# Position MLP of a four-layer conv/attention network: layer three in double calls, and one y word table written by halves

## The reference, cut to what matters

```
pos = grid_q[:, :, None, :] - grid_kv[:, None, :, :]          # 16 x 1024 x 64 x 2
bias = jnp.sign(pos) * jnp.log1p(jnp.abs(pos))
bias = jax.nn.relu(bias @ cpb_w1 + cpb_b1)                    # 2 -> 128
bias = jax.nn.relu(bias @ cpb_w2 + cpb_b2)                    # 128 -> 128
bias = (bias @ cpb_w3 + cpb_b3).reshape(b, GROUPS, H * W, Hd * Wd)   # 128 -> 1
sim = jnp.einsum('bhid,bhjd->bhij', qh, kh) + bias
```

## Time and profile before

| | us |
|---|---|
| median of three runs (2898.54 to 2902.41) | 2899.04 |
| time of the profiled execution | 2898.61 |
| its span, first to last instruction | 2896.8 |
| first y matmul of `stage_bias`, from the span's start | 131.0 |
| last layer-three matmul of `stage_bias` | 2038.4 |
| one group of 32 rows | 117.7 |

### The profile page before, as it was taken

One profiled execution on the slowest core, in us unless ns is written; L12 is line 12 of the kernel. 1 busy time (PEld: TensorE's weight loads), 2 busy tenths in 40 slices (PEclk: granted clock), 3 DMA queues, 4 the chain that ended last, 5 costly groups with the idle time before them and its releaser, 6 DMA issues. The chain is left out here.

```text
span 2896.8 us, 45091 instructions
## 1 busy us (share of the span) xinstructions
PE 2738.6 (95%) x19977; PEld 1342.3 (46%) x19977; DVE 2176.3 (75%) x1159; ACT 1650.0 (57%) x2588; POOL 100.8 (3%) x65
## 2 busy tenths in 40 slices
PE   7399999999999999999999999999799999999893
PEld 3333333333333333333333333333478888757551
DVE  5499999999999999999999999998542221234447
ACT  2466776767767777677676776766432222211335
POOL 0000000000000000000000000000422000000004
PEclk9699999999999999999999999999899999999997
DMA  1110000100001001000010000000600000200001
GB/s 68 40 38 14 23 22 16 34 14 23 29 11 34 21 16 36 14 23 22 17 34 14 23 29 10 27 5 1 192 1 0 1 0 1 83 0 1 1 1 58
DMA packets 37603, 72.21 MB, mean 25 GB/s; under 512 B 20960, under 2 KB 21920, under 8 KB 35744
## 3 DMA queue, kind: packets, MB, share of 16 engines
q1 hardware_dynamic: 37344, 69.19, 7.4%
q0 software_dynamic: 64, 0.13, 0.0%
HBM read 60.45 MB, written 8.86 MB: 24 GB/s over the span
## 5 line engine op out<-in xcount | busy, mean ns | idle before, releaser
L731 PE MATMUL l_ps<-mlp_w,W2H 128*64 128x512 f16 x8192 | 1369.1, 393 | 20.1 <-DVE mlp_w L760 20.1
L760 DVE TENSOR_TENSOR mlp_w<-words_x,words_y 128x4096 f32<-128x4096 f32 x256 | 1131.3, 4420 | 0.0
L803 ACT ACTIVATE mlp_w<-l_ps 128x512 f32<-128x512 f32 x1024 | 611.0, 597 | 470.2 <-PE l_ps L731 431.1
L731 PE MATMUL l_ps<-mlp_w,W2L 128*64 128x512 f16 x4096 | 804.0, 389 | 0.0
L731 PEld LDWEIGHTS l_ps<-mlp_w,W2H 128*64 128x64 f16 x8192 | 455.3, 108 | 555.0 <-issue 117.4
L748 DVE SCALAR_TENSOR_TENSOR mlp_w<-relu_bottom,sign_ratio,mlp_w 128x2048 f32<-128x2048 f32 x256 | 601.4, 2349 | 109.0 <-ACT relu_bottom L803 106.7
L803 ACT ACTIVATE relu_bottom<-l_ps 128x512 f32<-128x512 f32 x1024 | 613.0, 599 | 71.1 <-PE l_ps L731 1.4
L731 PEld LDWEIGHTS l_ps<-mlp_w,W2L 128*64 128x64 f16 x4096 | 228.9, 109 | 181.4 <-issue 0.7
L706 PE MATMUL l_ps<-mlp_w,W 128*32 128x512 f32 x2048 | 272.8, 605 | 2.1 <-DVE mlp_w L748 2.1
L719 PE MATMUL l_ps<-y_rows,y_weights_halves 12*128 12x512 bf16 x2048 | 202.5, 385 | 12.5 <-DMA y_rows<-y_pieces 12.5
L719 PEld LDWEIGHTS l_ps<-y_rows,y_weights_halves 12*128 12x128 bf16 x2048 | 51.6, 91 | 336.6 <-ACT relu_bottom L803 232.7
(11 more groups left out here) (339 smaller groups left out, 2410.0 us busy)
## 6 DMA issues: line engine op xcount, KB each, us to landing
table_pos<-pos_table SPq DMA_DIRECT2D x64, 512.0 KB, 3.7
mlp_w<-in_mlp_w SPq DMA_DIRECT2D x8, 1024.0 KB, 8.7
X<-in_x SPq DMA_DIRECT2D x8, 512.0 KB, 7.7
bias_scratch<-bias_rows SPq DMA_DIRECT2D x64, 64.0 KB, 2.0
mlp_w_hi<-bias_scratch SPq DMA_DIRECT2D x16, 256.0 KB, 6.7
out<-Q SPq DMA_DIRECT2D x8, 512.0 KB, 2.7
y_rows<-y_pieces SPq DMA_DIRECT2D x192, 12.0 KB
xn_b<-in_out_wT SPq DMA_DIRECT2D x1, 1024.0 KB, 8.4
```

Source lines behind the costliest of these rows:

```text
L731: last = nc.tensor.matmul(out[q][a * DH:(a + 1) * DH, :], w[:, half], h[a][:, :, k], start=False, stop=stop, tile_position=(0, a * DH))
L760: nc.vector.tensor_tensor(hw[i % 3].rearrange("p r (m j) -> p r m j", j=J), words_x.unsqueeze(1).to_broadcast([P, 2, W, J]), words_y[:, 2 ...
L803: nc.scalar.activation((tops, bots)[d][i % 2][:, r, BANK * u:BANK * (u + 1)], banks[BANK_OF[c % PER]][:], ACT.Relu).then_inc(relu, 1)
```

## The change: what it does

- PE calls layer three after each even pair but the first (after rows 1, 5, 9, ... of a `bg`) for the two pairs before it, instead of once after each odd row. `tops` has three buffers instead of two; the third takes the place in memory of a freed table.
- The x table still exists twice, the y table once. The first half of the y table (y rows 0 to 15) of the next `bg` is written after row 19 once `h1` of the first eight pairs is done; the second half after row 3 of the next `bg` itself. The x jobs come after rows 7 and 11. The `low` parts follow: `h1` pairs 6, 8, 12, and pair 4 of the next `bg`. DVE waits for three jobs at pair 0 and for the fourth at pair 8.
- ACT waits for layer three of pair `i - 3` before it writes a top buffer, and for the fold of pair `i - 2` before it writes a bottom buffer.
- SyncE issues the store of a group before, not after, job 0's coordinates and the y rows of the `bg` after next.

```diff
-    tab = [[sb(f"words_{a}{i}", [P, COLS]) for a in "xy"] for i in range(2)]
+    tab_x, tab_y = [sb(f"words_x{i}", [P, COLS]) for i in range(2)], sb("words_y", [P, COLS])
-    tops = [room([P, 2, TWO]) for _ in range(2)]
+    tops = [room([P, 2, TWO]) for _ in range(2)] + [sb("relu_top", [P, 2, TWO])[:]]
...
+    def words_of(bg, job):
+        a, half = divmod(job, 2)
+        return hi_lo((tab_y[:] if a else tab_x[bg % 2][:])[:, half * HALFC:(half + 1) * HALFC])
...
                     for job in range(1, JOBS):
                         coords(bg + 1, job)
+                store(bg)
                 if bg + 2 < BG:
                     coords(bg + 2, 0)
                     y_rows(bg + 2)
-                store(bg)
...
-                if r and i:
+                if r and i and i % 2 == 0:
+                    layer_three(i - 2)
                     layer_three(i - 1)
+            layer_three(DBL - 2)
             layer_three(DBL - 1)
...
-                    dve.wait_ge(words, JOBS * (bg + 1))
+                    dve.wait_ge(words, JOBS * bg + 3)
+                if n == PER_BG // 2:
+                    dve.wait_ge(words, JOBS * bg + 4)
...
-                if bg + 1 < BG and n >= 4 and n % 2 == 0 and n < 4 + 2 * JOBS:
-                    low(bg + 1, (n - 4) // 2)
+                if bg and n == 4:
+                    low(bg, 3)
+                if bg + 1 < BG and n in (6, 8, 12):
+                    low(bg + 1, (6, 8, 12).index(n))
...
-                if bg >= 2:
+                if a == 0 and bg >= 2:
                     act.wait_ge(h1, PER_BG * (bg - 1))
+                if a and bg:
+                    act.wait_ge(h1, PER_BG * bg - (PER_BG // 2 if half == 0 else 0))
...
-                    if r == 0 and q == 0 and i >= 2:
-                        act.wait_ge(l3, i - 1)
+                    if r == 0 and q == 0 and i >= 3:
+                        act.wait_ge(l3, i - 2)
+                    if r == 0 and q == 1 and i >= 2:
+                        act.wait_ge(folded, i - 1)
...
-                if bg + 1 < BG and y >= 3 and y % 4 == 3 and y < 3 + 4 * JOBS:
-                    high(bg + 1, (y - 3) // 4)
+                if bg and y == 3:
+                    high(bg, 3)
+                if bg + 1 < BG and y in (7, 11, 19):
+                    high(bg + 1, (7, 11, 19).index(y))
```

More of the change, by code:

```diff
@@ L705, in layer_three @@
                     r, u = divmod(q, 2)
-                    last = nc.tensor.matmul(p3[32 * q:32 * q + 32, :], K.W3[:, 30 - 2 * n:62 - 2 * n], tops[i % 2][:, r, BANK * u:BANK * (u + 1)],
+                    last = nc.tensor.matmul(p3[32 * q:32 * q + 32, :], K.W3[:, 30 - 2 * n:62 - 2 * n], tops[i % 3][:, r, BANK * u:BANK * (u + 1)],
                                             start=(n == 0), stop=(n == PER_BG - 1), tile_position=(0, 32 * q))
@@ L740, in low @@
             def low(bg, job):
-                a, half = divmod(job, 2)
                 dve.wait_ge(hi_done, JOBS * bg + job + 1)
-                w = hi_lo(tab[bg % 2][a][:, half * HALFC:(half + 1) * HALFC])
+                w = words_of(bg, job)
                 nc.vector.tensor_tensor(w[:, :, 0], val[:], w[:, :, 1], ALU.subtract).then_inc(words, 1)
@@ L747, in fold @@
                 dve.wait_ge(relu, 2 * CH * (i + 1))
-                nc.vector.scalar_tensor_tensor(tops[i % 2], bots[i % 2][:], K.RHO[:], tops[i % 2], ALU.mult, ALU.add).then_inc(folded, 1)
+                nc.vector.scalar_tensor_tensor(tops[i % 3], bots[i % 2][:], K.RHO[:], tops[i % 3], ALU.mult, ALU.add).then_inc(folded, 1)
             for job in range(JOBS):
@@ L757, in _ @@
                 if n == 0:
-                    dve.wait_ge(words, JOBS * (bg + 1))
-                words_x, words_y = (t[:].rearrange("p (m j) -> p m j", j=J) for t in tab[bg % 2])
+                    dve.wait_ge(words, JOBS * bg + 3)
+                if n == PER_BG // 2:
+                    dve.wait_ge(words, JOBS * bg + 4)
+                words_x, words_y = (t[:].rearrange("p (m j) -> p m j", j=J) for t in (tab_x[bg % 2], tab_y))
                 nc.vector.tensor_tensor(hw[i % 3].rearrange("p r (m j) -> p r m j", j=J),
@@ L780, in high @@
                 act.wait_ge(val_done, n + 1)
-                if bg >= 2:
+                if a == 0 and bg >= 2:
                     act.wait_ge(h1, PER_BG * (bg - 1))
-                nc.scalar.activation(hi_lo(tab[bg % 2][a][:, half * HALFC:(half + 1) * HALFC])[:, :, 1], val[:],
-                                     ACT.Copy, scale=BELOW).then_inc(hi_done, 1)
+                if a and bg:
+                    act.wait_ge(h1, PER_BG * bg - (PER_BG // 2 if half == 0 else 0))
+                nc.scalar.activation(words_of(bg, job)[:, :, 1], val[:], ACT.Copy, scale=BELOW).then_inc(hi_done, 1)
             def copy_rows(bg):
@@ L800, in _ @@
                     act.wait_ge(l2, c + 1)
-                    if r == 0 and q == 0 and i >= 2:
-                        act.wait_ge(l3, i - 1)
-                    nc.scalar.activation((tops, bots)[d][i % 2][:, r, BANK * u:BANK * (u + 1)], banks[BANK_OF[c % PER]][:], ACT.Relu).then_inc(relu, 1)
+                    if r == 0 and q == 0 and i >= 3:
+                        act.wait_ge(l3, i - 2)
+                    if r == 0 and q == 1 and i >= 2:
+                        act.wait_ge(folded, i - 1)
+                    nc.scalar.activation((bots[i % 2] if d else tops[i % 3])[:, r, BANK * u:BANK * (u + 1)], banks[BANK_OF[c % PER]][:], ACT.Relu).then_inc(relu, 1)
                     if bg and y == 2 and q == 0:
                         copy_rows(bg - 1)
-                if bg + 1 < BG and y >= 3 and y % 4 == 3 and y < 3 + 4 * JOBS:
-                    high(bg + 1, (y - 3) // 4)
+                if bg and y == 3:
+                    high(bg, 3)
+                if bg + 1 < BG and y in (7, 11, 19):
+                    high(bg + 1, (7, 11, 19).index(y))
             copy_rows(BG - 1)
```

## The result

The changed kernel takes 2908.1 us, the kernel before 2901.3 us (medians of ten runs each): ratio 1.0027, 95% interval 1.0018 to 1.0036 (ratio and interval are estimated from all ten runs of each; the medians alone give 1.0023). It is slower by about a quarter of a per cent, 6.8 us in the medians and 9.6 us between the spans of the profiled executions (2906.4 against 2896.8). I had forecast the right sign and 18.8 us, starting from 2899.0, the median of the first three runs of before; the size was too large, by a factor of 2.0 against the spans and of 2.8 against the medians.

The account below looks back on a forecast made before the run. PE was taken to set the pace, busy for all 117.70 us of a group. Stalls of 31.5 us less 12.7 saved by merging gave 18.8 us more, 2917.8 us, with a range from 2907 to 2931.

Parts of the forecast that it names:

- The stall: PE before y groups of rows 5, 9, 13, 21 waits for ACT's relu behind a table job: 31.5 us more.
- the bank rule: With 7 banks and 4 per row, row 5's last chunk needs the bank that row 4's first relu frees.
- The saving of the merging: Two layer-three calls in a row spare one change of shape: 127 x 0.10 = 12.7 us less.
- the upper bound: Saving per double layer-three call at most 0.13, if the second call is also spared the slower first step.
- its two rows of 7.33: Row 4 and the row before it on PE take 7.33 us; 16 x 7.33 = 117.3, nearly the group's 117.70.
- Banks free in time: Rival: row 4's first relu after a job ends by T+3.12, only the merging is left, 2886.3 us; 8%.
- Calls that don't chain: Rival: each of two successive layer-three calls ends as before, merging saves nothing, 2930.5 us; 7%.
- A stall that lasts to the next row: Rival: ACT or DVE don't catch up before row 6, twice the price, 2949 us; 4%.
- Half of the stall: Rival: table jobs get shorter or start earlier, ending within 0.2%, about 2902 us; 3%.
- Costs put at nothing: Single y table by halves, DVE's moved work, three top buffers with new waits, SP's queue order: cost 0 each.

Follow-up runs that it names:

- the two runs with other places: Changed kernel with table jobs after rows 4, 8, 12, 20, or after rows 6, 10, 14, 22: 2876.5 and 2915.3 us, one run each.
- the third call: Changed kernel with an extra layer-three call between the two of a double call, in 112 of 127 places: 3000.2 us in one run.
- The run with single calls: Changed kernel with layer three once per pair again, all else of the change kept: 2899.6 us, ratio 1.0001 to the kernel before.

## Why the prediction was right in its mechanism and wrong in its size

*The stall: right.* Predicted 0.56 and 0.49, 60 times, 31.5 us. Measured 0.54 (3.72 against 3.18) and 0.46 (3.64 against 3.18). By groups: 118.37 with the waits, 116.32 with the jobs elsewhere, so 2.05 in a group with four jobs, where 2.10 was forecast; over 15 groups' worth of jobs some 30.8. The traces have it directly too: the stage takes 1916.4 us in the changed kernel and 1885.8 with the jobs two rows later, 30.6 less. The 0.02 to 0.03 too much in each are a release of 0.05 instead of 0.06, a relu that ends at T+3.67 instead of T+3.68 and, for the y job, a row of 3.18 where I had taken 3.16. Its place, its count and its releaser are as forecast, and the two runs with other places show that the bank rule, not a rule of thumb on pauses, decides.

*The saving of the merging: the step that failed.* The prediction said "Inside a double call the 0.55 becomes a pass step of 0.45: 0.10 saved", and from it 12.7 us. The group without stalls measures 116.32 against 117.70: 1.38 us saved per group, not 0.80, so about 1.38 x 15.9 = 22 us (the stage itself: 1907.8 - 1885.8 = 22.0). It has two parts.
- The calls themselves: 2.00 became 1.86, 0.14 saved and not 0.10, which is 8 x 0.14 = 1.12 of the 1.38. The pass step that I took from the earlier trace rows, 0.45, was the step out of the first pass behind layer two; the steps between later passes are 0.42 to 0.43, in the double calls and in the third call alike. The passes of the double call on PE's timeline, looked at in short windows, start at 1000.92, 1001.38, 1001.80 and 1002.23, and the next y group at 1002.78: steps of 0.46 (0.45 in most double calls), 0.42, 0.43 and 0.55, where I had summed 0.45 three times and 0.55. I had named this very excess (0.03, from layer two's first step) and put it into the upper bound instead of the sum. The bound itself, 0.13, was too low by 0.01.

```profile
1001.38 0.61 PE L710 MATMUL l_ps<-mlp_w,W 128*32 128x512 f32 x4
1001.80 0.61 PE L710 MATMUL l_ps<-relu_top,W 128*32 128x512 f32 x4
...
1002.23 0.61 PE L710 MATMUL l_ps<-relu_top,W 128*32 128x512 f32 x4
```

- The rest, 1.38 - 1.12 = 0.26 per group or 0.03 per four rows, lies in the rows' layer two: before, every second even row took 3.22 and the odd row behind it 3.15 without its layer three; afterwards these two take 3.16 and 3.18. The kernel before:

```profile
1013.69 0.40 PE L719 MATMUL l_ps<-y_rows,y_weights_halves 12*128 12x512 bf16 x4
1016.91 0.39 PE L719 MATMUL l_ps<-y_rows,y_weights_halves 12*128 12x512 bf16 x4
```

  I had put this at nothing. The prediction had a sign of it: its two rows of 7.33 give 117.3 us for a group, and the group takes 117.70. The run with single calls has the 3.22 again with three top buffers, so it goes with the spacing of the layer-three calls. The excess is spread over the row's matmul steps, no single one is longer by more than 0.02, and no wait is shown. By what mechanism is open; no run was aimed at it.

So the sum is 30.6 - 22.0 = 8.6 us, which is what the stage grew by; it stands against 9.6 between the spans and 6.8 between the medians, and the interval (0.18% to 0.36%, 5.2 to 10.4 us) holds all three. With 0.14 in place of 0.10 the forecast would have been 31.5 - 17.8 = 13.7, and with the measured 22 it would have been 9.5. Two opposed terms of nearly one size make a small difference, and a saving put 9 us too low doubled the forecast.

*The rivals.* Banks free in time: no, the waits are there. Calls that don't chain: no, a double call takes 1.86 and not 2.00. The Trainium skill, TensorE: Matmul & The Clock Gate, in the list "What overlaps and what doesn't", has it that weight loads overlap matmuls in flight only if the row group differs. The trace of the changed kernel disagrees: the weights for the second call's first pass go in at 1001.38, when the first call's second pass has just started, and those for its second pass at 1001.81, when its first has, with no step of the matmuls longer for it and all in one row group:

```profile
1000.92 0.16 PEld L710 LDWEIGHTS l_ps<-mlp_w,W 128*32 128x32 f32 x8 [0.43 <-issue]
1001.38 0.13 PEld L710 LDWEIGHTS l_ps<-relu_top,W 128*32 128x32 f32 x4 [0.30 <-issue]
1001.81 0.13 PEld L710 LDWEIGHTS l_ps<-relu_top,W 128*32 128x32 f32 x4 [0.30 <-issue]
```

A stall that lasts to the next row: no, rows 6, 10 and so on are 3.16 to 3.18. Half of the stall: no; this rival's 3 us more lie nearer to the measured 7 to 10 than my 18.8, but the stalls have their full length. *Costs put at nothing* (DVE's load, the halves of the y table, the buffers' waits, SP's order): right, by the run with single calls; the one that was not nothing is the spacing of the rows above.

## What to carry to other kernels

A pause of a bounding engine may be paid-for cover for an engine that is far from full: before removing or moving one, list what runs on the others during it, and compute the due time of the first buffer behind it (here the first relu had to end within 3.12 us of the next row's start, and ended after 3.67). Price two opposed terms with the same care, and take a repeated step's cost from a step in the middle, not from the first one after a switch. If an occasional job of 2.5 us is too long for its gap, moving it to another gap or cutting it in two may cost nothing: here moving it by two rows turned a loss of 0.27% into a gain of 0.66%, by one row did as well in the groups, and by three rows made it worse (118.7 to 118.9 us a group), so the due time has to be worked out for each place.

## What the runs showed of the hardware that was not expected

- A change from one kind of matmul to another costs on both sides: 0.09 to 0.12 before the next group starts (0.55 after the last pass of layer three instead of 0.43, 0.32 after the last pair of layer two instead of 0.22 to 0.23) and 0.02 to 0.03 in the first step after it (0.45 to 0.46 instead of 0.43). Shape and element type change together here, and no run tells which of them it is. A float32 call of two passes costs 1.00 alone and 0.86 between two like it.
- Layer two's rows of one and the same work took 3.15 to 3.22 us, and their sum in a group moved by 0.26 us with the spacing of the layer-three calls; the reason is open.
